# Output and low-part stores of the apply stage moved from SyncE's queue to GpSimd's

## The chip, the cores and the metric

The kernel runs on one core of a Trainium2 chip. The metric is the time of one execution on the device in microseconds (us), as the median of several runs. A core has TensorE (matrix products, PE in the rows), VectorE (DVE), ScalarE (ACT), GpSimd (POOL) and SyncE (SP). DMAs are issued here by SyncE and by GpSimd; each issues in the order in which its program stands, and waits on semaphores in that order too.

## The reference, cut to what matters

x has 8 batches of 512 rows and 2048 columns. A linear layer with a LoRA part chosen per batch is followed by a second linear layer, whose weight is stored as 4-bit codes with a scale for each 64 elements:

```python
base = jnp.einsum('bsi,oi->bso', x, weight) + bias1
low = jnp.einsum('bsi,bri->bsr', x, lora_a[adapter_id])
delta = jnp.einsum('bsr,bor->bso', low, lora_b[adapter_id])
h = base + scale[:, None, None] * delta
w = (NF4[codes.reshape(-1)].reshape(-1, 64) * absmax[:, None]).reshape(codes.shape)
out = x + jnp.einsum('bsd,od->bso', h, w) + bias2
```

## The kernel before, in words

The two weights are first multiplied with each other, so that x is multiplied once. The kernel has a long first part (to about 918 us), in which the codes become numbers, the combined weight is made for four quarters of 512 output columns (NS = 4) and stored in DRAM (wc_d), and x is transposed and stored in DRAM (xc_d) in the seven combinations that a Strassen-like product needs.

The **apply stage** follows, and the change is in it alone. It runs over quarters j = 0 to 3 and in each over 16 pairs of 128-row blocks (PAIRS = 16), so over 64 pairs numbered 0 to 63 (pp). A pair consists of seven products f = 0 to 6 (A11, A12, S2, SS1, S3, S4, A22), written (pair, product) below. Odd quarters go through the pairs backwards, so that pair 16 has the same x as pair 15 and needs no x load. For each product:
- SyncE loads the x block into slot f (xr, `load_x`, L429) once the product that used that slot in the pair before has ended (semaphore product_done, s_prod).
- ScalarE writes its high part (L727) and VectorE its rest (L1014) into the same slot (xs), both five products ahead (LEAD = 5).
- TensorE multiplies (L1408 to L1412, or L1242 to L1244) into one of five PSUM banks, `bank_p[i % 5]`. It waits until the product five earlier has been added to the result (s_ev).
- VectorE adds the product to the result buffer `res` (L1060 to L1110).

`res` has two buffers, one for each pair in turn, with the two row blocks u = 0 and 1. It is first filled with x itself, the residual (`load_res`, L435), then takes the seven products, and then the LoRA part and biases for each u (TensorE L1290, VectorE L1117, semaphore lora_added, s_lev). After that each u is stored in the output (`store_out`, L442). `load_res(pp + 1)` waits until both stores of that buffer's pair before (pp - 1) have landed (out_stored, s_out).

In the first quarter the low part (x times LoRA A) of each 128-row block comes out beside products. It is put into one of four buffers `low_st` (VectorE L1031, semaphore low_stack_done) and stored in DRAM for the later quarters (`store_low`, L474). From pair 17 on it is read back (`load_low`, L469).

What sets the order: one program written by hand per engine. SyncE's loop over products i = (pp, f) is, in short: at each f wait for product i and load the x block of the next pair; at f = 2 store the second half of the pair before and, in the first quarter, a low part; at f = 3 load two low parts; at f = 4 load the residual of the next pair and, for odd pairs, the LoRA B parts (L454); at f = 6 store a low part and the first half of this pair. In pair 16 the store of f = 2 and the residual load of f = 4 both stand at f = 5. GpSimd issues small loads and 12 stores of early x blocks (L613) up to about 100 us and nothing after that.

Of the kernel before, what the change touches and what calls it, by code (L numbers as in the profile page):

```python
# [6 lines left out]
def adaln_ffn_kernel(  # L7
# [27 lines left out]
    F32, F32R, I32 = mybir.dt.float32, mybir.dt.float32r, mybir.dt.int32  # L35
    ALU, ACT = mybir.AluOpType, mybir.ActivationFunctionType
    P = 128
# [34 lines left out]
    SW = D // NS  # L72
# [14 lines left out]
    PAIRS = NB * S // P // 2  # L87
    ALL_PAIRS = NS * PAIRS
# [25 lines left out]
    def pieces_of(g):  # L114
        j, s = divmod(g, S1)
        if j == 0:
            return PIECES + s - (1 if s else 0) if s != 1 else None
        return PIECES * (j + 1) + s if j + 1 < NS and s < PIECES else None
# [16 lines left out]
    def low_slot(n):  # L135
        return n % 4 if n < 2 * PAIRS else (n + 2) % 4
# [13 lines left out]
    def groups_of(g):  # L150
        if not 1 <= g <= 2 * UNITS:
            return []
        return [i for i in ([2 * g - 2] if g % 2 else [2 * g - 3, 2 * g - 2, 2 * g - 1]) if i >= 4 * EARLY]
# [15 lines left out]
    def pair_at(pp):  # L169
        j, p = divmod(pp, PAIRS)  # L170
        return p if j % 2 == 0 else PAIRS - 1 - p
# [7 lines left out]
    def is_new(i):  # L179
        pp = i // NF  # L180
        return pp < PAIRS or pp % PAIRS != 0
# [17 lines left out]
    low_d = nc.dram_tensor("low_d", [2 * PAIRS, P, P], F32).ap()  # L199

    ctx = ExitStack()
    with ctx:
# [4 lines left out]
        def at(name, kb, shape, dt):  # L207
            return nc.alloc_sbuf_tensor_at(name, shape, dt, offset=base + int(kb * KB))
# [30 lines left out]
        res = [at(f"res{i}", 176 + 4 * i, [P, 2, SW], F32) for i in range(2)]  # L239
        g_raw = at("g_raw", 184, [P, SW], F32)  # L240
        g_b = [at(f"g_b{i}", 186 + 2 * i, [P, SW], F32R) for i in range(2)]
        low_st = [at(f"low_st{i}", 190 + 0.5 * i, [P, P], F32R) for i in range(4)]
# [94 lines left out]
        s_lst = sem("low_stack_done")  # L337
        s_lowst = [sem(f"low_stored{i}") for i in range(4)]
        s_lowld = [sem(f"low_loaded{i}") for i in range(4)]
        s_lora = sem("lora_multiplied")  # L340
        s_lev = sem("lora_added")
        s_res = [sem(f"res_loaded{i}") for i in range(2)]
        s_out = [sem(f"out_stored{i}") for i in range(2)]
# [4 lines left out]
        o_rows = out.rearrange("b s d -> (b s) d")  # L348

        @block.sync  # L350
        def _(sp):
# [72 lines left out]
            def load_comb(j, f):  # L424
                main = slice(R, R + HW) if f in WITH_LOW else slice(0, HW)
                sp.dma_start(cr[f][:, :, LO, main], wc_d[j, f]).then_inc(s_cld[f], 16)

            def load_x(pp, f):
                sp.dma_start(xr[f][:, LO, :, :], xc_d[pair_at(pp), f]).then_inc(s_xld[f], 16)  # L429
# [5 lines left out]
                sp.dma_start(res[pp % 2][:, :, :], x_rows[2 * p * P:2 * (p + 1) * P, j * SW:(j + 1) * SW]  # L435
                             .rearrange("(u p) o -> p u o", p=P)).then_inc(s_res[pp % 2], 16)

            def store_out(pp, u):
                j, p = pp // PAIRS, pair_at(pp)
                sp.wait_ge(s_lev, 2 * pp + u + 1)  # L440
                row = (2 * p + u) * P
                sp.dma_start(o_rows[row:row + P, j * SW:(j + 1) * SW], res[pp % 2][:, u, :]  # L442
                             ).then_inc(s_out[pp % 2], 16)

            def load_g(n):
                j, b = n // NB, batch_at(n)
                if n:
                    sp.wait_ge(s_gblo, n)
                else:
                    sp.wait_ge(s_gst, 16 * NS)  # L450
                    sp.wait_ge(s_btst, 16 * NS)
                    sp.wait_ge(s_zero, 1)
                for row in (0, 2 * R, 4 * R):
                    sp.dma_start(g_raw[row:row + R, :], g_d[j, b * R:(b + 1) * R, :]).then_inc(s_gld, 16)  # L454
                if n % NB == 0:
                    for row in (3 * R, 6 * R):
                        sp.dma_start(g_raw[row:row + 2, :], bt_d[j]).then_inc(s_gld, 16)
                        sp.dma_start(g_raw[row + 2:row + 3, :], bias2[j * SW:(j + 1) * SW]
                                     .rearrange("(a o) -> a o", a=1)).then_inc(s_gld, 16)
# [8 lines left out]
            def load_low(n):  # L468
                sp.dma_start(low_st[low_slot(n)][:, :].bitcast(F32), low_d[2 * pair_at(n // 2) + n % 2]  # L469
                             ).then_inc(s_lowld[low_slot(n)], 16)  # L470

            def store_low(n):
                sp.wait_ge(s_lst, n + 1)
                sp.dma_start(low_d[n], low_st[low_slot(n)][:, :].bitcast(F32)).then_inc(s_lowst[low_slot(n)], 16)  # L474

            load_codes(0)
            load_codes(1)
# [25 lines left out]
            for g in range(JOBS):  # L503
                j, s = divmod(g, S1)
# [34 lines left out]
                n, ahead = pieces_of(g), [i + 3 for i in groups_of(g) if i + 3 < 4 * UNITS]  # L539
# [31 lines left out]
            for i in range(PRODUCTS):  # L571
                pp, f = divmod(i, NF)
                j, p = divmod(pp, PAIRS)
                if pp + 1 < ALL_PAIRS:
                    sp.wait_ge(s_prod, i + 1)
                    if is_new(i + NF):
                        load_x(pp + 1, f)
                    if p == PAIRS - 1:
                        if f == 0:
                            sp.wait_ge(s_wst, 16 * HK * (j + 2))  # L580
                        load_comb(j + 1, f)
                if f == (5 if pp == PAIRS else 2) and pp:
                    store_out(pp - 1, 1)
                if f == 2 and 1 <= pp <= PAIRS:
                    store_low(2 * pp - 1)
                if f == 3 and PAIRS < pp < ALL_PAIRS - 1:
                    for u in range(2):
                        if pp <= PAIRS + 2:
                            sp.wait_ge(s_lowst[low_slot(2 * (pp + 1) + u)], 16 * (2 * PAIRS // 4))
                        n = 2 * (pp + 1) + u  # L590
                        sp.wait_ge(s_lora, n - 3)
                        load_low(n)
                if f == (5 if pp == PAIRS else 4) and pp and pp + 1 < ALL_PAIRS:
                    load_res(pp + 1)
                if f == 4 and p % 2 and pp + 1 < ALL_PAIRS:
                    load_g((pp + 1) // 2)
                if f == 5 and p % 2 == 0 and j == 0 and p + 2 < PAIRS:
                    load_a(p // 2 + 1)
                if f == 6:
                    if j == 0:  # L600
                        store_low(2 * pp)
                    store_out(pp, 0)
            store_out(ALL_PAIRS - 1, 1)
            for i in range(2):
                sp.wait_ge(s_out[i], 16 * ALL_PAIRS)

        @block.gpsimd
        def _(pool):
            def store_early(m):
                p, c = divmod(m, 2)  # L610
                pool.wait_ge(s_xcp, 4 * (m + 1))
                for u, f in ((slice(0, 2), slice(A11, S2)), (slice(2, 4), slice(S3, NF, 2))):
                    pool.dma_start(xc_d[p, f, :, c * QK:(c + 1) * QK, :].rearrange("f p k t -> p f k t"),  # L613
                                 x_early[m % RING][:, u, :, :]).then_inc(s_early[m % RING], 16)

            pool.dma_start(rank_c[:, :], rank_of).then_inc(s_small, 16)
            pool.dma_start(adapt_c[:, :], adapter_of).then_inc(s_small, 16)
            pool.dma_start(ids_i[:, :], itok.partition_broadcast(P)).then_inc(s_small, 16)
            pool.dma_start(scale_c[:, :], bass.AP(scaling.tensor, scaling.offset, [[1, NA], [0, R], [1, 1]])
                           ).then_inc(s_small, 16)  # L620
            pool.dma_start(b1_nat[:, :], bias1.rearrange("(t p) -> p t", p=P),
                           allow_slow_non_contiguous=True).then_inc(s_small, 16)
            pool.dma_start(a_nat[:, :], lora_a.rearrange("a r i -> (a r) i")).then_inc(s_a_nat, 16)
            for a in range(NA):
                pool.dma_start(b_cols[:, a * R:(a + 1) * R], lora_b[a]).then_inc(s_bcols, 16)
            store_early(0)
            pool.wait_ge(s_bcols, 16 * NA)
            for h in range(2):
                pool.dma_start(raw[h][:, LO, :, :], b_cols.rearrange("(k p) c -> p k c", p=P)[:, h * HK:(h + 1) * HK, :]
                               ).then_inc(s_b_ld[h], 16)  # L630
            for m in range(1, EARLY - 1):
                store_early(m)
            pool.wait_ge(s_a_raw, 1)
            pool.dma_start(a_sel_d.rearrange("b p f -> p b f"),
                           a_raw[:, :, :, :, :].rearrange("p b h k r -> p b (h k r)")).then_inc(s_a_st, 16)
            store_early(EARLY - 1)

        def evacs(g):
            return g - g // S1
# [816 lines left out]
```

## Time and profile before

| | us |
|---|---|
| median of 3 runs | 2225.14 |
| the three runs | 2223.64, 2225.14, 2225.20 |
| the profiled execution | 2223.64 |
| its span, first to last instruction | 2221.9 |
| mean granted clock of TensorE in it | 0.990 |

The profile is one execution. Its own time is the lowest of the three. Busy time says what an engine did; the waits say who let it go on. "SPq" rows are DMA issues in SyncE's queue; a row with x3 merges three issues, and its length is from the first to the last of them. A landing is the time from the issue of a DMA to the arrival of its last part.

### The profile page before, as it was taken

How to read it: one execution, taken by the hardware profiler on the slowest of the kernel's cores; microseconds unless marked ns; L12 is line 12 of the kernel's file. 1: busy time of each engine (PE TensorE's matmuls, PEld its weight loads, DVE VectorE, ACT ScalarE, POOL GpSimd, SP SyncE). 2: the span in 40 equal slices, each digit the busy share in tenths (PEclk: the TensorE clock that was granted, in tenths of full speed). 3: DMA queues.
4: the chain of work that ended last, by engine and by line, in shares of the span. 5: the costliest groups of instructions: out<-in, count | busy, mean ns of one | idle time of the engine just before them, and what ended most of it. 6: DMA issues, size and time to landing. Idle time of an engine off the chain costs nothing.

```text
span 2221.9 us, 31532 instructions
## 1 busy us (share of the span) xinstructions
PE 2166.7 (98%) x12104; PEld 1862.7 (84%) x12104; DVE 1789.5 (81%) x2655; ACT 1018.2 (46%) x1277; POOL 24.4 (1%) x33
## 2 busy tenths in 40 slices
PE   3799999999999999999999999999999999999999
PEld 3688778787878787899999988888988889888888
DVE  6899879868975574688887898888898887888887
ACT  6655555555554333444444434333444334443332
POOL 3100000000000000000000000000000000000000
PEclk7899999999999999999999999999999999999999
DMA  9587788887888897877777887787977778877775
GB/s 275 192 254 246 249 251 254 264 252 250 255 260 253 280 286 243 273 243 236 240 242 232 272 277 243 242 248 243 297 256 247 244 246 256 291 251 246 240 244 173
DMA packets 380948, 558.00 MB, mean 251 GB/s; under 512 B 23152, under 2 KB 234768, under 8 KB 380672
## 3 DMA queue, kind: packets, MB, share of 16 engines
q1 hardware_dynamic: 377712, 544.95, 77.3%
q0 software_dynamic: 3088, 11.03, 1.5%
q8 instruction: 98, 1.61, 0.3%
q14 instruction: 50, 0.41, 0.1%
HBM read 427.96 MB, written 128.99 MB: 251 GB/s over the span
## 4 chain that ended last, share of the span: by engine, by line
PE 95%; DMA 2%; ACT 1%; DVE 1%; issue 0%; SPq 0%; DVEq 0%; ACTq 0%
PE ps L1408 26%; PE ps L1242 15%; PE ps L1244 15%; PE ps L1243 15%; PE ps L1409 13%; PE ps L1412 4%; PE ps L1257 2%; PE ps L1411 2%; PE ps L1290 1%; DMA code_w<-in_L_ffn_codes_dram 1%; PE ps L1238 1%; DMA raw<-in_L_cond_weight_dram 0%; DMA xr<-xc_d 0%; ACT wq_nat_w L666 0%; ACT tile L685 0%
## 5 line engine op out<-in xcount | busy, mean ns | idle before, releaser
L1408 PE MATMUL ps<-comb,xs 128*128 128x512 f32 x2527 | 903.2, 395 | 0.0
L727 ACT CAST xs<-xr 128x1024 fp32r<-128x1024 f32 x427 | 449.7, 1054 | 623.3 <-DMA xr<-xc_d 622.7
L1409 PE MATMUL ps<-comb,xs 128*128 128x256 f32 x2527 | 707.8, 280 | 0.0
L1014 DVE TENSOR_TENSOR xs<-xr,xs 128x1024 fp32r<-128x1024 f32 x427 | 521.4, 1222 | 126.8 <-ACT xs L727 124.0
L1408 PEld LDWEIGHTS ps<-comb,xs 128*128 128x128 f32 x2527 | 474.3, 188 | 102.4
L1409 PEld LDWEIGHTS ps<-comb,xs 128*128 128x128 f32 x2527 | 475.4, 188 | 14.5
L1242 PE MATMUL ps<-wq,tile 128*128 128x512 f32 x1088 | 468.2, 430 | 3.9 <-DVE tile L948 3.9
L1244 PE MATMUL ps<-wq,tile 128*128 128x512 f32 x1088 | 427.4, 393 | 0.0
L1243 PE MATMUL ps<-wq,tile 128*128 128x512 f32 x1088 | 426.5, 392 | 0.0
L1242 PEld LDWEIGHTS ps<-wq,tile 128*128 128x128 f32 x1088 | 205.6, 189 | 71.5 <-DVE tile L948 3.7
L1244 PEld LDWEIGHTS ps<-wq,tile 128*128 128x128 f32 x1088 | 205.2, 189 | 45.1
L1243 PEld LDWEIGHTS ps<-wq,tile 128*128 128x128 f32 x1088 | 207.1, 190 | 25.7 <-issue 0.7
L1242 PE MATMUL ps<-comb,xs 128*128 128x272 f32 (+1 forms) x696 | 201.4, 289 | 0.9 <-issue 0.9
L1244 PE MATMUL ps<-comb,xs 128*128 128x272 f32 (+1 forms) x696 | 199.2, 286 | 0.0
L1243 PE MATMUL ps<-comb,xs 128*128 128x272 f32 (+1 forms) x696 | 198.6, 285 | 0.0
L685 ACT CAST tile<-raw 128x1024 fp32r<-128x1024 f32 x136 | 142.2, 1057 | 114.7 <-DMA raw<-in_L_cond_weight_dram 112.4
L948 DVE TENSOR_TENSOR tile<-raw,tile 128x1024 fp32r<-128x1024 f32 x136 | 162.2, 1221 | 37.1 <-ACT tile L685 36.8
L1412 PE MATMUL ps<-comb,xs 128*128 128x512 f32 x361 | 142.4, 394 | 0.0
L1242 PEld LDWEIGHTS ps<-comb,xs 128*128 128x128 f32 x696 | 131.0, 188 | 3.5 <-issue 1.3
L1243 PEld LDWEIGHTS ps<-comb,xs 128*128 128x128 f32 x696 | 131.0, 188 | 1.0
L1244 PEld LDWEIGHTS ps<-comb,xs 128*128 128x128 f32 x696 | 130.9, 188 | 0.0
L654 ACT ACTIVATE wq_nat<-wq_nat,consts 128x512 f32<-128x512 f32 x156 | 113.4, 727 | 4.9
(119 smaller groups left out, 2199.8 us busy)
## 6 DMA issues: line engine op xcount, KB each, us to landing
xr<-xc_d SPq DMA_DIRECT2D x427, 512.0 KB, 4.0
raw<-in_L_cond_weight_dram SPq DMA_DIRECT2D x128, 512.0 KB, 4.4
xc_d<-rq SPq DMA_DIRECT2D x26, 1792.0 KB, 7.5
res<-in_x_dram SPq DMA_DIRECT2D x64, 512.0 KB, 5.4
out_dram<-res SPq DMA_DIRECT2D x128, 256.0 KB, 4.5
wc_d<-cs SPq DMA_DIRECT2D x32, 896.0 KB, 4.7
comb_raw<-wc_d SPq DMA_DIRECT2D x28, 1024.0 KB, 7.7
x_nat<-in_x_dram SPq DMA_DIRECT2D x104, 256.0 KB, 3.9
```

The costliest lines, as they stand in the source:

```text
L654: nc.scalar.activation(wq_nat[nat_slot(n)][:, :], src[:, :], ACT.Prelu, bias=bends[i], scale=1.0 if i else RISE, alpha=SLOPES[i]).then_inc ...
L685: nc.scalar.copy(tile[slot][:, HI, :, :], raw[slot][:, LO, :, :]).then_inc(s_hi, 1)
L727: nc.scalar.copy(xs[f][:, HI, :, :], xr[f][:, LO, :, :]).then_inc(s_xhi, 1)
L948: tt(tile[slot][:, LO, :, :], raw[slot][:, LO, :, :], tile[slot][:, HI, :, :].bitcast(F32), ALU.subtract).then_inc(s_lo, 1)
L1014: tt(xs[f][:, LO, :, :], xr[f][:, LO, :, :], xs[f][:, HI, :, :].bitcast(F32), ALU.subtract).then_inc(s_xlo, 1)
L1242: nc.tensor.matmul(out_ap, t_hi, m_hi, start=first, stop=False)
L1243: nc.tensor.matmul(out_ap, t_hi, m_lo, start=False, stop=False)
L1244: return nc.tensor.matmul(out_ap, t_lo, m_hi, start=False, stop=last)
L1257: ins = nc.tensor.transpose(tr_x[i % 2][:, t * P:(t + 1) * P], src[:, t * P:(t + 1) * P], ident[:, :])
L1408: nc.tensor.matmul(bank[:, :], x_hi, both, start=(k == 0), stop=False)
L1409: nc.tensor.matmul(bank[:, 0:HW], x_lo, high, start=False, stop=False)
L1412: last = nc.tensor.matmul(bank[:, :], x_hi, both, start=False, stop=True)
```

## The change

`store_out` and `store_low` with their waits move from SyncE's program to GpSimd's, at the end of it, in a loop of their own. SyncE keeps all loads of the apply stage, the waits of the residual loads for the stores, and the last wait for all stores. The diff, cut:

```diff
@@ SyncE's program
-            def store_out(pp, u):
-                j, p = pp // PAIRS, pair_at(pp)
-                sp.wait_ge(s_lev, 2 * pp + u + 1)
-                row = (2 * p + u) * P
-                sp.dma_start(o_rows[row:row + P, j * SW:(j + 1) * SW], res[pp % 2][:, u, :]
-                             ).then_inc(s_out[pp % 2], 16)
-            def store_low(n):
-                sp.wait_ge(s_lst, n + 1)
-                sp.dma_start(low_d[n], low_st[low_slot(n)][:, :].bitcast(F32)).then_inc(s_lowst[low_slot(n)], 16)
...
-                if f == (5 if pp == PAIRS else 2) and pp:
-                    store_out(pp - 1, 1)
-                if f == 2 and 1 <= pp <= PAIRS:
-                    store_low(2 * pp - 1)
...
-                if f == 6:
-                    if j == 0:
-                        store_low(2 * pp)
-                    store_out(pp, 0)
-            store_out(ALL_PAIRS - 1, 1)
             for i in range(2):
                 sp.wait_ge(s_out[i], 16 * ALL_PAIRS)
@@ GpSimd's program
+            def store_out(pp, u):
+                j, p = pp // PAIRS, pair_at(pp)
+                pool.wait_ge(s_lev, 2 * pp + u + 1)
+                row = (2 * p + u) * P
+                pool.dma_start(o_rows[row:row + P, j * SW:(j + 1) * SW], res[pp % 2][:, u, :]
+                             ).then_inc(s_out[pp % 2], 16)
+            def store_low(n):
+                pool.wait_ge(s_lst, n + 1)
+                pool.dma_start(low_d[n], low_st[low_slot(n)][:, :].bitcast(F32)).then_inc(s_lowst[low_slot(n)], 16)
...
             store_early(EARLY - 1)
+            for pp in range(ALL_PAIRS):
+                if 1 <= pp <= PAIRS:
+                    store_low(2 * pp - 1)
+                if pp:
+                    store_out(pp - 1, 1)
+                if pp < PAIRS:
+                    store_low(2 * pp)
+                store_out(pp, 0)
+            store_out(ALL_PAIRS - 1, 1)
```

TensorE's, VectorE's and ScalarE's programs stay the same. The first place is SyncE's queue in pair 16, product 3 to pair 17, product 3, at the change from the first quarter to the second. Before, with xr the x blocks, res the residual and out_0_dram the output:

```order
L429 DMA xr3_122<-xc_d 128x1024 [waits product_done]
L429 DMA xr4_123<-xc_d 128x1024 [waits product_done]
L429 DMA xr5_124<-xc_d 128x1024 [waits product_done]
L442 DMA out_0_dram<-res1_127 128x512 [waits lora_added]
L435 DMA res1_127<-in_x_dram 128x2x512 [waits out_stored1]
L429 DMA xr6_125<-xc_d 128x1024 [waits product_done]
L442 DMA out_0_dram<-res0_126 128x512 [waits lora_added]
L429 DMA xr0_119<-xc_d 128x1024 [waits product_done]
L429 DMA xr1_120<-xc_d 128x1024 [waits product_done]
L429 DMA xr2_121<-xc_d 128x1024 [waits product_done]
L442 DMA out_0_dram<-res0_126 128x512 [waits lora_added]
L429 DMA xr3_122<-xc_d 128x1024 [waits product_done]
```

The same place of SyncE's queue now:

```order
L429 DMA xr3_122<-xc_d 128x1024 [waits product_done]
L429 DMA xr4_123<-xc_d 128x1024 [waits product_done]
L429 DMA xr5_124<-xc_d 128x1024 [waits product_done]
L435 DMA res1_127<-in_x_dram 128x2x512 [waits out_stored1]
L429 DMA xr6_125<-xc_d 128x1024 [waits product_done]
L429 DMA xr0_119<-xc_d 128x1024 [waits product_done]
L429 DMA xr1_120<-xc_d 128x1024 [waits product_done]
L429 DMA xr2_121<-xc_d 128x1024 [waits product_done]
L429 DMA xr3_122<-xc_d 128x1024 [waits product_done]
```

The three stores are gone from between the loads; the residual load still waits until the store has landed, and xr6 still stands behind it. The second place is GpSimd's queue, at the end of the first quarter, where it had no instruction before (low_d holds the low parts):

```order
L605 DMA low_d<-low_st2_133 128x128 [waits low_stack_done]
L600 DMA out_0_dram<-res1_127 128x512 [waits lora_added]
L605 DMA low_d<-low_st3_134 128x128 [waits low_stack_done]
L600 DMA out_0_dram<-res1_127 128x512 [waits lora_added]
L600 DMA out_0_dram<-res0_126 128x512 [waits lora_added] x2
L600 DMA out_0_dram<-res1_127 128x512 [waits lora_added] x2
```

These are the stores in the order in which their data come ready, a low part and an output half in turn in the first quarter and output halves alone afterwards. The third place is the end of SyncE's queue, before:

```order
L435 DMA res1_127<-in_x_dram 128x2x512 [waits out_stored1]
L429 DMA xr5_124<-xc_d 128x1024 [waits product_done]
L429 DMA xr6_125<-xc_d 128x1024 [waits product_done]
L442 DMA out_0_dram<-res0_126 128x512 [waits lora_added] x2
L442 DMA out_0_dram<-res1_127 128x512 [waits lora_added] x2
L202 UNCONDITIONAL_BRANCH [waits out_stored1,out_stored0]
```

Now the four stores are GpSimd's last ones, and SyncE goes from the last x load straight to the wait for them:

```order
L435 DMA res1_127<-in_x_dram 128x2x512 [waits out_stored1]
L429 DMA xr5_124<-xc_d 128x1024 [waits product_done]
L429 DMA xr6_125<-xc_d 128x1024 [waits product_done]
L202 UNCONDITIONAL_BRANCH [waits out_stored1,out_stored0]
```

What moved is the issuing engine alone: the kernel still ends when both stores of each buffer have landed.

## Rows read from the trace of the kernel before

**Rows 1.** The page's head and its busy time by engine.
```profile
span 2221.9 us, 31532 instructions
...
PE 2166.7 (98%) x12104; PEld 1862.7 (84%) x12104; DVE 1789.5 (81%) x2655; ACT 1018.2 (46%) x1277; POOL 24.4 (1%) x33
```

**Rows 2.** Windows: stretch, length, busy of PE, PEld, DVE, ACT, POOL, clock, DMA.
```profile
960.00:1265.00 305.00, 305.00 (x2158) 288.11 (x2158) 243.25 (x375) 137.79 (x194) 0.00 (x0) 1.00 0.78 249
1265.00:1581.00 316.00, 316.00 (x1861) 278.22 (x1860) 270.15 (x397) 126.57 (x132) 0.00 (x0) 1.00 0.80 252
```

**Rows 3.** Waits of PE from 500 us on: sum, times, longest.
```profile
PE ps L1279 <- DVE low_rep L1093: 1.2, 1, 1.2
PE ps L1242 <- issue: 0.9, 1, 0.9
```

**Rows 4.** Waits of SyncE's queue from 1080 us on.
```profile
SPq L429 <- PE ps L1412: 591.2, 297, 2.7
SPq L442 <- DVE res L1117: 106.5, 31, 10.7
...
SPq L435 <- DMA out_dram<-res: 6.6, 9, 1.8
```

**Rows 5.** Timeline of SyncE in a steady pair: start, length, instruction.
```profile
1401.06 0.43 SPq L442 DMA_DIRECT2D out_dram<-res  x1
...
1403.85 0.91 SPq L469 DMA_DIRECT2D low_st<-low_d  x2
...
1406.67 0.44 SPq L435 DMA_DIRECT2D res<-in_x_dram  x1
...
1423.98 0.90 SPq L469 DMA_DIRECT2D low_st<-low_d  x2
```

**Rows 6.** Landing of the 427 x loads (tile xr).
```profile
DMA to landing us min/median/max: 3.0/4.0/10.4
```

**Rows 7.** Timeline of SyncE from pair 16, product 5 on.
```profile
1274.72 0.34 SPq L442 DMA_DIRECT2D out_dram<-res  x1
1276.87 0.39 SPq L435 DMA_DIRECT2D res<-in_x_dram  x1
1277.31 0.66 SPq L429 DMA_DIRECT2D xr<-xc_d  x1
...
1278.89 2.00 SPq L429 DMA_DIRECT2D xr<-xc_d  x3
```

**Rows 8.** Timeline of ScalarE there: product (17,0) taken, then x of (17,6).
```profile
1274.08 0.37 ACT L764 COPY u_sum<-ps 128x256 f32<-128x256 f32 x1 [1.66 <-PE ps L1412]
1283.48 1.05 ACT L727 CAST xs<-xr 128x1024 fp32r<-128x1024 f32 x1 [9.03 <-DMA xr<-xc_d]
```

**Rows 9.** Timeline of VectorE there: sums of (17,0), (17,1) and (17,2).
```profile
1281.80 0.42 DVE L1060 TENSOR_TENSOR u_sum<-ps,u_sum 128x256 f32<-128x256 f32 x1 [1.32 <-DMA res<-in_x_dram]
...
1286.16 0.42 DVE L1071 TENSOR_TENSOR res<-ps,res 128x256 f32<-128x256 f32 x1
...
1289.34 0.43 DVE L1080 TENSOR_TENSOR res<-u_sum,res 128x256 f32<-128x256 f32 x1
```

**Rows 10.** GpSimd's stores L613 with landings, then the landing of its L616.
```profile
L613 POOL DMA_DIRECT2D xc_d<-x_early x12: 710/722/1010, 35.1 to 99.5; - x12
...
DMA to landing us min/median/max: 3.2/6.4/9.7
...
DMA to landing us min/median/max: 3.0/3.0/3.0
```

**Rows 11.** The last store's issue, then the landings of all 128 output stores.
```profile
2219.39 0.33 SPq L442 DMA_DIRECT2D out_dram<-res  x1
...
DMA to landing us min/median/max: 2.0/4.5/7.1
```

**Rows 12.** GpSimd's issues at the start, and VectorE's L929 (min/median/max ns).
```profile
5.51 7.27 POOL L625 DMA_DIRECT2D b_cols<-cond_lora_b_weights_dram  x7
...
L929 DVE TENSOR_TENSOR low_tw<-low_tw,low_uw x6: 1224/1225/1226, 7.2 to 65.2; 128x1024 f32<-128x1024 f32 x6
```

## The prediction, made before the change had run

> **What bounds the kernel now.** I read the page's busy line first, then busy time by stage, then what TensorE waited for, then what SyncE's queue waited for, and then three places in order of time. TensorE is busy 2166.7 us of a span of 2221.9 [rows 1]. In the apply stage, where all the moved instructions stand, its busy time equals the window: 305.00 of 305.00 us in the first quarter's stretch, 316.00 of 316.00 in the second, at a granted clock of 1.00 [rows 2]. After 500 us TensorE waits twice, 1.2 and 0.9 us, the first for a sum of VectorE, the second for nothing the profile names [rows 3]. So no transfer decides an instant of the apply stage as it stands. An edit of queues can cost time here if it lets a transfer come so late that TensorE starts to wait. It can give back 2.1 us at the very most, and no SyncE transfer is named in those.
>
> SyncE's queue is idle nearly always and waits to be allowed: from 1080 us on it waits 591.2 us for TensorE's products before x loads, and 106.5 us in 31 waits before an output store, the longest 10.7 [rows 4]. While it waits for such a store, the loads behind it are held. That is the only thing the change removes.
>
> **Steady pairs.** A pair takes 20.13 us (the two low-part loads at 1403.85 and 1423.98), and 1401.06 to 1406.67 is two products, so a product takes 2.8 us and a LoRA product (20.13 - 7 x 2.8) / 2 = 0.26 [rows 5]. An x block is asked for when its slot's product ends, and is used one pair later less one product: 20.13 - 2.8 = 17.3 us. Landing takes 4.0 at the median [rows 6], ACT's cast 1.05 [rows 8] and VectorE's difference about 1.2 (the longest kind, rows 12 have one of the same size). That is 6.3 us, so x has 11 us to spare. What the change does here:
> - Removed from SyncE: 128 output stores and 32 low-part stores with their waits. Loads go out earlier by up to the wait. Since TensorE waits for no load, worth 0.
> - Added to GpSimd: the same 160 issues. Its nearest row takes 0.71 to 1.01 us each [rows 10], so 2 per pair cost 1.4 to 2.0 us of an engine that is otherwise idle here (0.00 busy in rows 2), 4 per pair in the first quarter 2.8 to 4.0 of about 21. Worth 0 by themselves. The order on GpSimd is the order in which the sums come ready, so a store waits for no later one.
> - The residual load waits for the store of the buffer's other half: issued 1401.06, asked for at 1406.67 [rows 5]. A store that lands later than 5.6 us after its issue now holds SyncE, and the load of product 5 behind it. From GpSimd the nearest landing is 3.2 / 6.4 / 9.7 us (min / median / max, 512 KB, while much else moved), 3.0 for 8 KB in a quiet queue [rows 10]. At 6.4 SyncE waits 0.8 us per pair, at 9.7 it waits 4.1. Against 11 us to spare: 0.
>
> **The one tight place** is the change from the first to the second quarter. Pair 16 uses pair 15's x blocks again, its store and residual load both come at product 5. SyncE stores at 1274.72, the store lands and lets the residual load go at 1276.87 (2.15 us), and the x block of pair 17, product 6 goes behind it at 1277.31 [rows 7]. That block's slot was free since 1274.08 - 2.8 = 1271.3, the end of product (16,6). It reaches ACT at 1283.48 [rows 8]. VectorE waits for the residual until 1281.80, then has no gap that could absorb a delay: it ends the sum of (17,1) at 1286.58 and that of (17,2) at 1289.77 [rows 9]. A bank is used again five products later. Product (17,0) ended at 1274.08 [rows 8], so (17,6) starts at 1274.08 + 5 x 2.8 + 2 x 0.26 = 1288.6 and (18,0) at 1291.4. To spare: 2.0 us and 1.6 us. Behind the store stand the residual load, one x load, three more x loads. Whatever the GpSimd store adds to 2.15 us comes straight onto this chain, and 1.6 us of it is free. By the quiet rows of GpSimd, 3.0 and 3.2 [rows 10], it adds about 1.0: cost 0. By its median of 6.4 it adds 4.25: cost 2.65. I take 1.0, because this store too has a quiet queue (2.15 us from SyncE is near the 2.0 of the last store, rows 11). In the other two changes of quarter the residual load comes after the x loads that now go free of the store, so they gain room.
>
> **The end.** TensorE's last product is followed by three VectorE sums; SyncE issues the last store at 2219.39, and its landing is the 2.0 us minimum [rows 11]. The span ends at 2221.9, 0.5 us after. From GpSimd the smallest landings are 3.0 and 3.2 us [rows 10]; 256 KB lies between their sizes. Taking 3.1, the end comes 1.1 us later. The bounds are 1.0 (no GpSimd row lands in under 3.0, which excludes a gain) and 4.4 (the median 6.4). I take 1.1, since nothing else moves at the end. The Trainium skill, "DMA: Bandwidth & Descriptors", Specifications, gives the first byte at about 1 us on the GpSimd path against 0.6 on the other; by that alone the end would cost 0.4 us and the sum would be 0.7 us lower, and no run here has shown that pair of figures.
>
> **Sum.** 0 (steady) + 0 (tight place) + 1.1 (end) on the profiled execution's 2223.64 us gives 2224.7. That execution is the lowest of the three; the median is 1.5 higher at 2225.14, so the median forecast is 2226.2. What lies around the span (1.7 us) I leave as it is.
>
> **VectorE against GpSimd.** While GpSimd issued seven DMAs from 5.51 to 12.78 us, VectorE's tensor_tensor with two inputs in SBUF, first at 7.2, took 1224 to 1226 ns in all six cases [rows 12]. So an issue seems not to slow such an instruction. The Trainium skill, "SBUF — State Buffer", Who interferes with whom, says that VectorE in a two-port mode and GpSimd exclude each other for a whole instruction, that tensor_tensor has no such mode, and that with two SBUF inputs it contends only with GpSimd's reads. By that rule the trace agrees for this row; an exclusion, if it applied, is priced in rival 3.
>
> **Rivals.**
> 1. The store from GpSimd lands late in the tight place. It must add more than 1.6 us. At 6.4 us: 2.65 + 1.1 = 3.75, so 2228.9. For it: the median of rows 10. Against it: those were 512 KB each, in pairs, in a busy time.
> 2. The same chain, later still; this one ends on the other side. The slowness passes 0.2% (4.45 us on the median) when the tight place costs over 4.45 - 1.1 = 3.35, so when the landing exceeds 2.15 + 1.6 + 3.35 = 7.1 us. At the 9.7 us maximum of rows 10 it costs 9.7 - 2.15 - 1.6 = 5.95, with the end 7.05, so 2232.2. For it: such a landing exists in rows 10. Against it: it is the largest of twelve.
> 3. GpSimd's issues stop VectorE for their length. In steady pairs VectorE has (316.00 - 270.15) / 15.7 = 2.9 us free per pair and (305.00 - 243.25) / 14.5 = 4.3 in the first quarter [rows 2], against 2 x 0.72 = 1.4 and 4 x 0.72 = 2.9: hidden. In the tight place two issues fall on a VectorE without a gap: 1.0 + 1.4 - 1.6 = 0.8, plus 1.1: 1.9, so 2227.1. Against it: rows 12.
> 4. The freed loads gain something. TensorE's waits after 500 us are 2.1 us in all [rows 3]; with 1.1 for the end, 1.0 less than before: 2224.1. It can't reach 0.2%.
> 5. The change does nothing that shows, because the stores land as fast from GpSimd: 2225.1.
>
> **Chances.** Forecast 0.58; rival 1 0.12; rival 2 0.06; rival 3 0.08; rival 4 0.05; rival 5 0.09; 0.02 for something else. A measurement of this kernel can tell about 0.2% (4.45 us) from no change. Forecast and rivals 1, 3, 4, 5 all lie within it, so same 0.91; slower 0.07 (rival 2 and half of the rest); faster 0.02 for the rest. Eight in ten: from 2223.6, the lowest run of before, which takes in rivals 4 and 5, to 2229.5, which takes in rival 1 and the end's upper bound of 4.4 (2225.14 + 4.4 = 2229.5).
>
> **What would show it.** In the profile of the changed kernel: TensorE's busy time still fills the apply windows; SyncE's waits for VectorE's sum are gone and its waits for the output store grow from 6.6 us in 9 [rows 4] to some 20 to 60; GpSimd has 160 more issues of 0.7 to 1.0 us; the last store lands about 3.1 us after its issue; VectorE's wait for the residual near 1281 grows from 1.3 to about 2.3 us, and TensorE does not wait between 1288 and 1300. A TensorE wait there is rival 1 or 2, tensor_tensor above 1.23 us is rival 3. The forecast is wrong if TensorE waits at each pair, which would need a store to land over 16 us after its issue (5.6 and 11 to spare), or if TensorE's count of products in a stretch of rows 2 drops while it stays busy.

## The result and the profile after

| | before | the change |
|---|---|---|
| median of 7 runs, us | 2225.20 | 2232.28 |
| lowest to highest | 2223.64 to 2226.09 | 2229.87 to 2232.79 |
| span of the profiled execution | 2221.9 | 2230.9 |

The ratio is 1.0027, with a 95% interval of 1.0018 to 1.0036: slower by 7.1 us at the medians. That is 0.3% of the time, small but clear of the interval. The forecast was 2226.2 with a range up to 2229.5; the time lies above it.

The apply stage is not where it went. Windows of the changed kernel, with the columns of [rows 2]:

```profile
1265.00:1290.00 25.00, 25.00 (x144) 21.77 (x143) 20.11 (x30) 9.75 (x11) 1.52 (x3) 1.00 0.64 225
1290.00:1581.00 291.00, 291.00 (x1720) 256.45 (x1719) 249.43 (x367) 118.44 (x122) 15.83 (x30) 1.00 0.78 254
1581.00:1898.00 317.00, 317.00 (x1855) 278.44 (x1853) 271.67 (x396) 130.41 (x135) 16.81 (x31) 1.00 0.78 254
```

TensorE fills each window as before, the tight place at 1265 to 1290 included. Its waits from 500 us on, as in [rows 3]:

```profile
PE ps L1279 <- DVE low_rep L1093: 1.6, 2, 1.2
PE ps L1242 <- issue: 1.0, 1, 1.0
PE ps L1408 <- DVE comb L1008: 0.8, 1, 0.8
PE ps L1279 <- DVE low_rep L1067: 0.8, 1, 0.8
```

That is 4.2 us against 2.1. The two new ones of 0.8 us stand here in the timeline, next to GpSimd's first moved store:

```profile
923.99 0.33 PE L1279 MATMUL ps<-ident,low_rep 128*128 128x128 f32 x1 [0.82 <-DVE low_rep L1067]
930.96 0.50 PE L1408 MATMUL ps<-comb,xs 128*128 128x512 f32 x1 [0.82 <-DVE comb L1008]
...
933.99 0.56 POOL L605 DMA_DIRECT2D low_d<-low_st  x1 [834.61 <-DVE low_st L1031]
```

Both come before the first moved instruction, so the change can't have made them; they came back in a kernel in which no store moves (third experiment).

Now the end. The last sum of VectorE and the last store, and then two engines' rows at the end of their programs (line L202, the end of the kernel; duration in ns, then start). In these traces each engine's program ends with a row called DRAIN:

```profile
2220.64 0.69 DVE L1117 TENSOR_TENSOR res<-ps,res 128x512 f32<-128x512 f32 x1
2221.62 0.54 POOL L600 DMA_DIRECT2D out_dram<-res  x1 [2.50 <-DVE res L1117]
...
L202 POOLq EVENT_SEMAPHORE  x2: 17/17/17, 2230.7 to 2230.8; - x2
...
L202 POOLq DRAIN  x1: 9054/9054/9054, 2221.6 to 2221.6; - x1
...
L202 SPq DRAIN  x1: 7/7/7, 2224.2 to 2224.2; - x1
```

SyncE was through its last wait and its own DRAIN at 2224.2: every store had landed. GpSimd's DRAIN had begun with its last issue at 2221.6 and took 9.05 us; only at 2230.7 did GpSimd report, and the kernel ended. In the kernel before the same rows read:

```profile
L202 POOLq EVENT_SEMAPHORE  x2: 17/17/17, 2221.7 to 2221.8; - x2
L202 POOLq DRAIN  x1: 9328/9328/9328, 99.2 to 99.2; - x1
...
L202 SPq DRAIN  x1: 7/7/7, 2221.6 to 2221.6; - x1
```

A DRAIN of 9.33 us was there too, at 99.2 us, where GpSimd's program was at its end and nobody waited for it. From the start of the last sum to the end of the span is 2221.9 - 2218.67 = 3.2 us before and 2230.9 - 2220.64 = 10.3 after: 7.0 us more, nearly the whole of the 7.1 between the medians. (The two profiled spans differ by 9.0 us. The other 2.0 lie ahead of the last sum, and its start differs by more than that among the kernels below: from 2216.7 to 2223.5 in all but the last.)

### The profile page after: what moved, and what is told of

Read it like the earlier page. It is cut to its first block, busy times and chain, and to the rows that moved or that the text cites. A ratio compares the mean times of both kernels' runs of the same rounds, so it can differ in the third digit from the quotient of the medians.

```text
span 2230.9 us, 31532 instructions
## 1 busy us (share of the span) xinstructions
PE 2166.0 (97%) x12104; PEld 1861.1 (83%) x12104; DVE 1789.9 (80%) x2655; ACT 1018.5 (46%) x1277; POOL 110.8 (5%) x193
## 3 DMA queue, kind: packets, MB, share of 16 engines
q0 software_dynamic: 14352, 46.70, 5.8%
## 4 chain that ended last, share of the span: by engine, by line
PE 94%; DMA 2%; ACT 1%; DVE 1%; issue 1%; SPq 0%; POOLq 0%; POOL 0%; DVEq 0%; ACTq 0%
PE ps L1408 26%; PE ps L1242 15%; PE ps L1244 15%; PE ps L1243 14%; PE ps L1409 13%; PE ps L1412 4%; PE ps L1257 2%; PE ps L1411 2%; PE ps L1290 1%; DMA code_w<-in_L_ffn_codes_dram 1%; PE ps L1238 1%; DMA xr<-xc_d 0%; DMA raw<-in_L_cond_weight_dram 0%; ACT wq_nat_w L666 0%; DMA comb_raw<-wc_d 0%
## 5 line engine op out<-in xcount | busy, mean ns | idle before, releaser
L1014 DVE TENSOR_TENSOR xs<-xr,xs 128x1024 fp32r<-128x1024 f32 x427 | 521.3, 1221 | 122.2 <-ACT xs L727 119.5
L600 POOL DMA_DIRECT2D out_dram<-res x128 | 69.4, 542 | 1096.0 <-DVE res L1117 1086.8
```

The source lines that it names most:

```text
L600: pool.dma_start(o_rows[row:row + P, j * SW:(j + 1) * SW], res[pp % 2][:, u, :]).then_inc(s_out[pp % 2], 16)
L1014: tt(xs[f][:, LO, :, :], xr[f][:, LO, :, :], xs[f][:, HI, :, :].bitcast(F32), ALU.subtract).then_inc(s_xlo, 1)
```

## The experiments

**Theory D**: the cost is GpSimd's DRAIN, exposed because its last DMA is now the kernel's last. **Rival Q**: a queue of its own costs time spread over the apply stage, and the profile's end is chance. In f1, f2, f4, g1, g2, h1, i1 and i2, `by_pool(pp, u)` says in the diffs which output stores GpSimd issues; SyncE has the others and the low parts. The diffs are cut: the semaphores that a moved store needs are left out. The DRAIN rows are always those of the line where the kernel ends: duration in ns three times (min, median, max of one), then the start in us. Each DRAIN is read from one trace of its kernel.

### The last three stores back to SyncE (e1)

```diff
 GpSimd:
-            for pp in range(ALL_PAIRS):
+            for pp in range(ALL_PAIRS - 1):
...
-            store_out(ALL_PAIRS - 1, 1)
 SyncE:
+                if pp == ALL_PAIRS - 1 and f == 2:
+                    store_out(pp - 1, 1)
...
+            store_out(ALL_PAIRS - 1, 0)
+            store_out(ALL_PAIRS - 1, 1)
```

> All stores from GpSimd as in the change, except the last three (second half of pair 62, both halves of pair 63), which SyncE issues. Theory D (GpSimd's DRAIN at the end of its program, 9.05 us in the profile of the change, begins at its last issue and holds the end): GpSimd's last issue is now near 2199 us, the drain is over near 2209, long before the last store; median back at 2225.2, within 1.5. Rival Q (the stores in a queue of their own, with later landings and issues beside VectorE, cost time spread over the apply stage; 157 of 160 stay): median stays at 2230 or more.

Measured: 2224.84 us (10 runs) against 2225.09 (31 runs), ratio 1.0002 (0.9992 to 1.0011). The DRAIN is there at its full length, but over at 2210.1, where the span ends at 2226.0:

```profile
L202 POOLq DRAIN  x1: 8809/8809/8809, 2201.3 to 2201.3; - x1
...
L202 SPq DRAIN  x1: 7/7/7, 2225.5 to 2225.5; - x1
```

SyncE's DRAIN is shown for when SyncE had seen all stores landed. With 157 of the 160 moved stores still on GpSimd the loss is gone. Rival Q, which wanted 2230 or more, falls as the cause of the 7.1 us; the interval leaves room for a spread cost of up to 2.4 us.

### Only the last store from GpSimd (e2)

The kernel before, with one store moved:

```diff
 SyncE:
-            store_out(ALL_PAIRS - 1, 1)
 GpSimd:
             store_early(EARLY - 1)
+            pool.wait_ge(s_lev, 2 * ALL_PAIRS)
+            pool.dma_start(o_rows[row:row + P, (NS - 1) * SW:NS * SW], res[pp % 2][:, u, :]).then_inc(s_end, 16)
```

> The kernel before with only its very last output store issued by GpSimd. Theory D: the whole cost of the change from one store: the last store ends its issue at about 2220.2, the drain takes 9.05 from there, so the span is 2229.3 to 2229.5 where it was 2221.9; median 2225.2 + 7.1 = 2232.3. Rival Q: only that store's landing, 1 us or less: 2226.2.

Measured: 2225.17 us (10 runs) against 2225.09, ratio 1.0007 (0.9997 to 1.0016). Theory D had expected 7 us, and was wrong about this kernel: one late DMA does not bring a DRAIN of 9 us. The timeline of GpSimd, and the end:

```profile
2219.22 0.57 POOL L641 DMA_DIRECT2D out_dram<-res  x1 [2121.52 <-DVE res L1122]
...
L202 POOLq DRAIN  x1: 3093/3093/3093, 2219.2 to 2219.2; - x1
...
L202 SPq DRAIN  x1: 7/7/7, 2221.8 to 2221.8; - x1
```

3.1 us from the issue, and SyncE saw the store landed after 2.6: the DRAIN holds the end by 0.5 us. From the start of the last sum (2218.23) to the end of the span is 4.3 us, 1.0 more than before; the times of the runs can't show so little.

### GpSimd only waits (e3)

```diff
 GpSimd:
             store_early(EARLY - 1)
+            pool.wait_ge(s_lev, 2 * ALL_PAIRS)
```

> The kernel before, all stores from SyncE; GpSimd issues nothing more, but ends its program with a wait for VectorE's last sum. Theory D in its form D1 (the drain takes some 9 us whenever it starts): it starts at 2219.4, so the span is 2228.7 and the median 2232.1. Form D2 (the 9 us belong to a DMA issued by GpSimd shortly before): nothing to drain, median 2225.2. Rival Q: 2225.2.

Measured: 2225.42 us (10 runs) against 2225.09, ratio 1.0002 (0.9992 to 1.0011). The DRAIN shrinks to 1.4 us:

```profile
L202 POOLq DRAIN  x1: 1375/1375/1375, 2219.5 to 2219.5; - x1
```

In its waits of TensorE both of the change's new small waits are there, one line further down in the code, although no store has moved:

```profile
PE ps L1280 <- DVE low_rep L1068: 1.3, 1, 1.3
...
PE ps L1409 <- DVE comb L1009: 0.8, 1, 0.8
```

So the DRAIN has no fixed length; form D1 falls. GpSimd had issued 29 DMAs in this kernel, the same 29 as in the kernel before, where the DRAIN took 9.33 us. There it began while the last two stores of early x were being issued:

```profile
98.77 1.42 POOL L613 DMA_DIRECT2D xc_d<-x_early  x2 [5.97 <-ACT x_early L709]
```

Such a store landed after 6.4 us at the median [rows 10]. Whether its landing made up the 9.33 us no run shows, but the number of DMAs did not: with the same 29, long landed, it is 1.4.

### The very last store back to SyncE (e4)

The change, with `store_out(ALL_PAIRS - 1, 1)` alone in SyncE's program.

> All stores from GpSimd except the very last one, which SyncE issues. Theory D: GpSimd's last issue is the first half of pair 63, by the trace of before's times at 2216.4 + 0.3 + 0.54 = 2217.2; with 9.05 of drain the span ends at 2226.5 instead of 2221.9: median 2225.2 + 4.6 = 2229.8, or 2.5 less than with all stores from GpSimd. Rival Q: as the change, 2232.3, or 1 less at most.

Measured: 2229.11 us (10 runs) against 2225.09, ratio 1.0017 (1.0008 to 1.0026): 4.0 us, where 4.6 was worked out.

```profile
L202 POOLq DRAIN  x1: 8682/8682/8682, 2215.9 to 2215.9; - x1
...
L202 SPq DRAIN  x1: 7/7/7, 2220.7 to 2220.7; - x1
```

The DRAIN ends at 2224.6, 3.9 us after SyncE was ready: the end follows the start of GpSimd's DRAIN, 0.2 us behind the start of its last issue, plus 8.7 us. Together with e1 this shows the cause of the 7.1 us: GpSimd's DRAIN behind the last store. What is left is what makes the DRAIN 9 us long here and 3 us in e2.

### The last four and the last sixteen stores from GpSimd (f1, f2)

```diff
+    def by_pool(pp, u):
+        return pp >= ALL_PAIRS - 2
```

and `ALL_PAIRS - 8` in f2.

> The kernel before with its last four output stores (pairs 62 and 63) issued by GpSimd. DRAIN lasted 1.4 us with no late GpSimd DMA, 3.1 with one, about 9 with many. Theory C (each DMA that GpSimd issued in the stretch before adds its share, (3.1 - 1.4) = 1.7 us): 1.4 + 4 x 1.7 = 8.2 us, median 2225.1 + 6.2 = 2231.3. Theory T (only DMAs of the last few us count, stores here lie 2.5 to 11 us apart): two count, 4.8 us, median 2225.1 + 2.8 = 2227.9. Theory S (the size of the whole program's use of GpSimd's queue decides): 3.1 us as with one, median 2225.2.

> The kernel before with its last sixteen output stores (pairs 56 to 63) issued by GpSimd. Theory C: above 9 us if nothing limits it (28 us by the count); if it stops at about 9, median 2232.2. Theory T: 4.8 us, as with the last four. Theory S: 3.1 us, or little more.

Measured: f1 2226.53 us and f2 2225.93 (10 runs each) against 2225.60 (20 runs); ratios 1.0003 (0.9994 to 1.0013) and 1.0007 (0.9997 to 1.0016). The DRAINs, of f1:

```profile
L208 POOLq DRAIN  x1: 3182/3182/3182, 2224.5 to 2224.5; - x1
```

and of f2:

```profile
L208 POOLq DRAIN  x1: 3661/3661/3661, 2218.5 to 2218.5; - x1
```

Theory C (1.7 us for each recent DMA) and theory T (two count) both fall; theory S had forecast 3.1 us, or little more, and that came true. Sixteen late DMAs add 0.6 us to what one costs.

### GpSimd waits for its landings before it ends (f3)

```diff
 GpSimd, at the end of the change's program:
+            for i in range(2):
+                pool.wait_ge(s_out[i], 16 * ALL_PAIRS)
```

> The change, with one thing added: GpSimd waits until all its output stores have landed before its program ends, some 2.3 us after the last issue. Theory A (the drain is a waiting for the DMAs in flight): it shrinks to 1.4 us, over at about the landing, and the median is 2225.1 + 1 to 2 = 2226.6. Theory B (work that GpSimd does anyway in its own time after the issue): it shrinks by 2.3 us to 6.7, same end, median 2232.3. Theory C' (work that the drain itself starts): it stays 9 us and begins 2.3 us later, median 2234.6.

Measured: 2232.68 us (5 runs) against 2225.60, ratio 1.0034 (1.0021 to 1.0047).

```profile
L202 POOLq DRAIN  x1: 8481/8481/8481, 2221.1 to 2221.1; - x1
...
L202 SPq DRAIN  x1: 7/7/7, 2221.1 to 2221.1; - x1
```

The profile decides against theories A and B: all stores had landed at 2221.1 and the DRAIN began only then, and it still took 8.5 us. It is not a waiting for DMAs in flight and not work that GpSimd does beforehand. Theory C' stands: from the start of the last sum (2217.61) to the end of the span it is 12.2 us, where the change had 10.3. The time alone can't tell 2232.3 from 2234.6.

### A gap of 306 us before the last store (f4)

```diff
+        return pp < 3 * PAIRS or (pp, u) == (ALL_PAIRS - 1, 1)
```

> GpSimd issues the output stores of the first three quarters (96 of 128), SyncE those of the last quarter except the very last store, which GpSimd issues after 320 us without a DMA of its own. Theory C or T with recent DMAs alone: the drain is 3.1 us as with one late store, span at most 1 us over before's. Theory S (total use in the program): 9 us, span 7 us over before's.

Measured in one run: 2232.76 us, span 2231.0. The timeline of GpSimd, and the end:

```profile
2221.79 0.54 POOL L658 DMA_DIRECT2D out_dram<-res  x1 [305.94 <-DVE res L1140]
...
L208 POOLq DRAIN  x1: 8972/8972/8972, 2221.8 to 2221.8; - x1
```

306 us without a DMA don't shorten it: with one late store and 96 before the gap it takes 9.0 us, with one late store alone (e2) 3.1. What GpSimd's queue did earlier in the program counts.

### Between 45 and 126 DMAs, and small ones (g1, g2, g3)

g1 and g2 have `pp >= ALL_PAIRS - 16` and `pp >= ALL_PAIRS - 28`. g3 is e2 with 127 small stores ahead:

```diff
 GpSimd:
+            for n in range(2 * ALL_PAIRS - 1):
+                pool.wait_ge(s_lev, n + 1)
+                pool.dma_start(tiny_d[n], ident[0:16, 0:4]).then_inc(s_tiny, 16)
+            pool.wait_ge(s_tiny, 16 * (2 * ALL_PAIRS - 1))
```

> The kernel before with its last 32 output stores from GpSimd, so 61 GpSimd DMAs in all. DRAIN lasted 3.1, 3.2, 3.7 us with 30, 33, 45 DMAs of GpSimd in the program, and 9.0 to 9.1 with 126 and 189. Theory S1 (it grows with the DMAs issued since the program's start and stops at about 9): on the way, 4.3 us at 0.04 us per DMA. Theory S2 (it jumps once the queue's room has been used up once): 3.7 to 4.3 or 9, nothing between.

> The same with the last 56 output stores from GpSimd, 85 DMAs in all. Theory S1: 5.3 us at 0.04 per DMA (3.7 + 40 x 0.04), or up to 6.3 on the line from 45 to 126 DMAs. Theory S2: 5.3 or below, or 9, with g1 on the same line or already at 9.

> The kernel before with its last output store from GpSimd, and in front of it 127 GpSimd stores of 16 rows of 16 bytes into a scratch tensor, one at each sum that releases an output store; the output stores otherwise stay with SyncE. 157 GpSimd DMAs, but 2 KB of rows each instead of 256 KB. If the number of DMAs decides, the drain is about 9 us as in the change and the span 7 us over before's. If the rows or bytes that GpSimd's queue described decide, it is about 3.1 us as with one late store, and the span is within 1 us of before's.

One run each: 2229.46, 2229.65 and 2234.02 us, the kernel before at 2227.97 beside them. The DRAINs, of g1:

```profile
L208 POOLq DRAIN  x1: 4559/4559/4559, 2222.9 to 2222.9; - x1
```

of g2:

```profile
L208 POOLq DRAIN  x1: 6437/6437/6437, 2221.2 to 2221.2; - x1
```

and of g3:

```profile
L203 POOLq DRAIN  x1: 11144/11144/11144, 2220.9 to 2220.9; - x1
```

A steady growth, 0.1 us above the upper line of g2's expectation. A small store carries 16 rows of 16 bytes, 256 bytes in all and not the 2 KB that the expectation names at its end, yet 157 DMAs of which 127 are so small have a longer DRAIN than the change. From e2 to g3 it grows by (11.1 - 3.1) / 127 = 0.063 us for each small store. From f2 to g2 it grows by (6.4 - 3.7) / 40 = 0.069 for each large one. So up to here the number of DMAs decides, and not their bytes.

### All 128 output stores, low parts left with SyncE (h1)

`by_pool` is always true; `store_low` stays in SyncE's program.

> All 128 output stores from GpSimd, the 32 low-part stores left with SyncE: 157 GpSimd DMAs, as many as in the kernel with tiny stores, whose drain took 11.1 us, against 9.1 with 189 in the change. Theory N (their number alone decides, and something clears or reuses a part between 157 and 186): 11.1 us, span 9 us over before's, median 2225.5 + 9 = 2234.5. Theory L (large stores stop at 9 us, at 126 as at 189): 9.0 us, median 2232.4. Either way the cost is at the end alone, and taking the low parts out of GpSimd's queue does not save the change.

Measured: 2225.59 us (10 runs) against 2226.39 (13 runs), ratio 1.000 (0.9991 to 1.001).

```profile
L208 POOLq DRAIN  x1: 3009/3009/3009, 2217.7 to 2217.7; - x1
```

Both theories missed: 157 DMAs, and a DRAIN of 3.0 us. The last sentence of the expectation missed too, for with the low parts left to SyncE the loss is gone. The ten runs agree with the one trace: with a DRAIN of 9 us in all of them the median would be near 2232. So all 128 output stores can come from GpSimd, the last one too, at no cost that the runs show (the interval is 0.1%, or 2.2 us). In the trace the end is 1.0 us longer than before: 4.2 us from the start of the last sum (2216.69) to the end of the span.

### Number against reuse of the queue's room (i1, i2, i3)

Theory W: the DRAIN works off what was issued since the queue's room was last reused, and rows use the room up. Theory X: the number of DMAs decides, going up and down.

```diff
 i1, GpSimd, beside the 128 output stores:
+                    if pp < PAIRS:
+                        pool.wait_ge(s_lst, 2 * pp + u + 1)
+                        pool.dma_start(tiny_d[2 * pp + u], ident[0:16, 0:4]).then_inc(s_tiny, 16)
 i2:
+        return pp >= 8
 i3, GpSimd, in g3's loop:
+                for m in range(2):
+                    pool.dma_start(tiny_d[2 * n + m], ident[0:16, 0:4]).then_inc(s_tiny, 16)
```

> All output stores from GpSimd, low parts with SyncE as in the run before (drain 3.0 us with 157 DMAs), and in the first quarter 32 GpSimd stores of 16 rows of 16 bytes into a scratch tensor at the low parts' times: 189 DMAs, as many as in the change, whose drain took 9.1. Theory W (the drain works off the DMAs issued since the queue's room was last reused, 0.067 us each; room is used up by rows, and the small stores use next to none): the reuse lies where it lay, near the end, so the drain stays 3 to 4 us and the span within 1 us of before's. Theory X (the number of DMAs decides, going up and down with it): 9 us, span 7 us over before's.

> The last 112 output stores from GpSimd, 141 DMAs; with 126 the drain was 9.0, with 157 it was 3.0. Theory W: either no reuse yet, then 9.0 + 15 x 0.067 = 10.0 us, or just after one, about 3. Saturation at 9 us, the other reading of 126 and 189 DMAs, gives 9.0.

> As the kernel with 127 tiny GpSimd stores (157 DMAs, drain 11.1 us), but two of them each time: 254 tiny ones, 284 DMAs. Theory W: the small stores don't use up the room, so the drain goes on growing: 11.1 + 127 x 0.067 = 19.6 us, span 15 us over before's. If a limit by number exists, 11 or less.

One run each: 2232.11, 2231.99 and 2239.79 us, the kernel before at 2226.32 beside them. The DRAINs, of i1:

```profile
L209 POOLq DRAIN  x1: 8562/8562/8562, 2221.5 to 2221.5; - x1
```

of i2:

```profile
L208 POOLq DRAIN  x1: 9786/9786/9786, 2220.2 to 2220.2; - x1
```

and of i3:

```profile
L203 POOLq DRAIN  x1: 11066/11066/11066, 2226.7 to 2226.7; - x1
```

i1 has the change's number of DMAs with 32 small ones for its 32 low parts, and the change's DRAIN within 0.5 us: theory W, which kept it at 3 to 4 us, falls, and small DMAs count like the low parts. That small stores use next to no room, as theory W took it, isn't shown: in the queue's packets 32 of them are 1024, as many as 32 low parts. Counted so, the reuse would lie 13 output stores earlier (80 packets each) and the DRAIN would be 3.0 + 13 x 0.067 = 3.9 us, so W falls by this measure too. i2, and g3 more clearly, speak against a stop at 9 us. i3 has twice the small stores of g3 and the same DRAIN; between 157 and 284 DMAs it did not grow. Theory X fits i1, but the two kernels with 157 DMAs, at 3.0 and 11.1 us, refute it. (i3's last sum began at 2225.43, later than in any other kernel here, 2216.7 to 2223.5; why isn't known, so its DRAIN says more than its time.)

All together, in order of the number of DMAs that GpSimd issued in the whole program:

| GpSimd DMAs | kernel | DRAIN, us |
|---|---|---|
| 29, DRAIN at the last of them (99.2 us) | before | 9.3 |
| 29, none late | e3 | 1.4 |
| 30 | e2 | 3.1 |
| 33 | f1 | 3.2 |
| 45 | f2 | 3.7 |
| 61 | g1 | 4.6 |
| 85 | g2 | 6.4 |
| 126 | f4 | 9.0 |
| 141 | i2 | 9.8 |
| 157, 128 of them output stores | h1 | 3.0 |
| 157, 127 of them small stores | g3 | 11.1 |
| 186 to 189 | e1, e4, the change, f3, i1 | 8.5 to 9.1 |
| 284, 254 of them small stores | i3 | 11.1 |

From 45 to 141 DMAs it grows by (9.8 - 3.7) / 96 = 0.064 us per DMA. Beyond that it is no function of the number alone: 157 gives 3.0 and 11.1. The packets of GpSimd's queue, which the page of each profile counts in its third part, don't order the lines either: 7232 in g3 (11.1 us), 11296 in i3 (11.1), 12048 in i2 (9.8), 13328 in h1 (3.0), 14352 in i1 and the change (8.6 and 9.1). **This stays open.** A reuse of the queue's room somewhere past i2's 141 DMAs would explain h1, but not that 32 small stores more bring back 8.6 us in i1. What would explain all the lines I don't know.

## Why the prediction was wrong, point by point

- **What bounds the kernel**: right. TensorE fills the apply stage before and after.
- **Steady pairs, cost 0**: right, within what the runs can tell; e1 has 157 moved stores at a ratio of 1.0002, h1 128 at 1.000. The sizes were kinder than forecast. GpSimd issues a store in 0.54 us, not 0.71 to 1.01, and the stores land sooner than SyncE's did. The output tensor's view in the change (issues in ns, landings in us):

```profile
L600 POOL DMA_DIRECT2D out_dram<-res x128: 540/542/553, 941.2 to 2221.6; - x128
...
DMA to landing us min/median/max: 2.3/3.5/7.0
```

  The median was 4.5 us before [rows 11]. SyncE's wait for landed stores from 1080 us on grew from 6.6 us [rows 4] to 41.1, inside the forecast 20 to 60, and TensorE waited for none of the loads behind it. The waits of SyncE's queue in the change:

```profile
SPq L429 <- PE ps L1412: 684.9, 314, 2.7
...
SPq L435 <- DMA out_dram<-res: 41.1, 9, 7.8
```

- **The tight place, cost 0**: right. The chain of [rows 7 to 9] in the change, as GpSimd's store, SyncE's residual load and VectorE's sum:

```profile
1275.88 0.54 POOL L600 DMA_DIRECT2D out_dram<-res  x1 [15.31 <-DVE res L1117]
...
1278.19 0.38 SPq L435 DMA_DIRECT2D res<-in_x_dram  x1
...
1283.66 0.42 DVE L1060 TENSOR_TENSOR u_sum<-ps,u_sum 128x256 f32<-128x256 f32 x1 [2.30 <-DMA res<-in_x_dram]
```

  The store lets the load go after 2.3 us; VectorE's wait is the 2.3 us that were forecast, and TensorE has none there. Rivals 1 and 2 did not happen: they needed a landing here of more than 3.75 and 7.1 us.
- **VectorE against GpSimd (rival 3)**: did not happen. VectorE's tensor_tensor L1014 had a mean of 1222 ns before and kept it beside 160 issues (the page's groups; busy us, mean ns):

```profile
L1014 DVE TENSOR_TENSOR xs<-xr,xs 128x1024 fp32r<-128x1024 f32 x427 | 521.3, 1221 | 122.2 <-ACT xs L727 119.5
```

- **The end, 1.1 us: this step failed**, by 5.9 us. It took the landing of the last store for what ends the span, and the rest, 0.5 us, as fixed. In its place the runs show GpSimd's DRAIN, 9.05 us from the last issue, which outlasts the landing by far: 7.0 us more at the end instead of 1.1. The landing itself was put too high: the store lands 2.3 us after its issue, not 3.1, against 2.0 from SyncE, and the lower bound of 1.0, which "excludes a gain", had no more to stand on than rows of other sizes. These rows have 0.3 us between the two landings, and GpSimd's issue comes 0.3 us behind the sum (2220.64 + 0.69 to 2221.62), where SyncE's came at once. The Trainium skill, "DMA: Bandwidth & Descriptors", Specifications, gives the first byte at about 1 us on the GpSimd path and 0.6 on the other, 0.4 apart; the landings come near that difference, and no run here shows the first byte.

  The span ends when every engine's program has ended, and not, as the section on the change says, when the stores have landed. Moving the last DMA to GpSimd moved the DRAIN from 99.2 us to the end. Its row, 9.33 us long, stood in the trace of before on the line of the kernel's end, and the prediction did not read that line; "What lies around the span (1.7 us) I leave as it is" looked only outside the span. The row should have raised a rival. It could not have given the size. Taken as it stands it makes 9.33 from the last issue, less the 2.5 us from the last issue to the end of before: 6.8, so 2232.0. That this meets the measured time is luck: with the same 29 DMAs the DRAIN of e3 took 1.4 us, and the same sum for e2 and h1, where GpSimd also issues the last store, would have been wrong by some 6 us (DRAINs of 3.1 and 3.0). In those two kernels the end is 1.0 us longer than before, near the 1.1 of the forecast.
- **The sign**: slower beyond 0.2% had a chance of 0.07, of which 0.06 stood for rival 2, a late landing that did not happen, and 0.01 for something unnamed. No rival named the end of GpSimd's program. (The chances for same, slower and faster have a slip: forecast and rivals 1, 3, 4 and 5 add up to 0.92, not 0.91.)

## What to carry to other kernels

An engine's program has an end, and the kernel waits for all of them. Before an engine that finished early gets the last instruction of a kernel, look at what follows its last instruction now, on the line where the kernel ends. What stands there is a warning and not a price: the row of before had 9.33 us, and at the end of the kernel GpSimd's DRAIN took from 1.4 to 11.1. The remedy that was shown is one of order: let GpSimd issue the others, and give the last stores to a queue whose end is short (SyncE's DRAIN took 7 ns). Three were enough here, with the DRAIN over 16 us before the end (e1); one was too few (e4). Leaving the low parts with SyncE removed the loss as well (h1), but no run shows why, and with 32 small stores added it came back (i1), so it is nothing to build on. None of these kernels is faster than the one before.

## What the runs showed of the hardware that was not expected

- GpSimd's DRAIN right behind a DMA of its own at the end of the kernel took 3.0 to 11.1 us. It grew by 0.064 us per DMA issued in the program from 45 to 141 of them, and by 0.063 per small store from 30 to 157. A pause of 306 us did not take it below 9.0 us (f4), and when it began after every DMA had landed it was 0.6 us shorter (8.5 against 9.05). Why it was 3.0 us with 157 DMAs of which 128 are output stores is open.
- The other engines' programs end with a DRAIN too. In the trace of the change TensorE's took 3.5 us, ScalarE's 1.1 and VectorE's 0.7, all over before the last store had landed, and SyncE's 7 ns.
- Output stores of 256 KB landed after 3.5 us at the median from GpSimd's queue and 4.5 from SyncE's. In f3, h1 and i1, where GpSimd also issues all 128, the medians were 4.0, 3.8 and 4.2. No run separates the queue from the moment of issue.
